# A graph layer on one core: the last slot keys turned in the feature split, dense work from the first group

## The chip, the cores and the metric

One core of one Trainium2 chip runs the kernel. The metric is the device time of one execution in microseconds; of several executions the median is given.

## What is computed

A graph network layer over 12,500 nodes of 128 features and 200,000 edges that are sorted by destination. Each edge has a source, a destination and one of nine types. `_layernorm` subtracts the mean of a row and divides by its standard deviation.

```python
src_h = h[src] @ W_msg.T + b_msg
msg = src_h + edge_embed[clip(edge_type, 0, 8)]
messages = segment_sum(msg, dst, num_segments=12500)
h_new = gru_cell(messages, h, W_ih, W_hh, b_ih, b_hh)
out = _layernorm(x + h_new)
```

Destinations are drawn as 12500 times the square of a uniform number, so low nodes have many edges each and high nodes few.

## The kernel before

The kernel sums raw features (and counts of types) per destination first and applies the weights to the sums. It has two ways to sum, by destination.

**The sparse way** serves nodes from 3584 up. Its edges come as 736 tiles of 128, in 184 groups of four. GpSimd gathers the source rows of a tile from memory by an indirect DMA (L604) into a ring of 23 tiles, and waits on `s_used` for the tile that stood in the slot. VectorE builds a one-hot of destinations and one of types (L844, L846), TensorE multiplies both with the gathered rows into one PSUM bank `psg` (L1061 for groups below 22, L1065 after, then L1069), and VectorE adds the bank into a ring of sums (L891). Group g + 1 may write `psg` only once that addition of group g is through.

**The dense way** serves nodes below 3584. All features stay in SBUF as three bf16 parts, `xs`. The edges are cut into 1748 slots of 128 edges of a few nodes. A slot has three keys per edge: `lo` and `key` (in `prm`) and `sort`. From them VectorE builds one-hots for four slots at a time (L862, L865, L868), TensorE multiplies them into `psb` (a "B" item, L1082), ScalarE copies each finished PSUM bank, four nodes wide, to SBUF (L1213), and for a finished block of 128 nodes TensorE multiplies the matrix with `xs` (an "F" item, L1097, in 49 parts of two matmuls).

**The split phase** stands ahead of both: 25 units of four feature tiles, each passing TensorE (L970, L973, L979) and ScalarE (L1147, L1153) in turn, give `xs`. SyncE writes `xs` out as `x_split` (L546) when the flag is known, for the gathers of the later groups. Beside the units VectorE finds the slots' edges, and `dense_keys(k)` (L688 to L698) makes the keys of a piece of slots: pieces 0 and 1 hold four columns of 128 slots, piece 2 holds six. TensorE turns keys by matmuls with an identity, `turn(a)` at L992, four columns at a time, the fourth time two. ScalarE copies what is turned from PSUM (`turned(a)`, L1163 and L1166). Turns 0 and 1 follow units 15 and 18. A matmul at L1002, after unit 21, adds up what VectorE has checked; VectorE makes the `flag` of it (L750 to L752), and every engine reads it before the main phase begins.

**The order of the main phase** is a list, `ITEMS`, which `schedule()` writes in Python and which TensorE, VectorE and ScalarE each walk. It puts one "G" and one "GA" item per group, and dense units between them so far as their share of the total keeps behind `pace((g - LEAD) / (GROUPS - REST - LEAD))`, from group `LEAD` on. With `LEAD = 4` the first B stands in group 4, one of 1748, and the first F in group 9. The item "keys" (piece 2) stands ahead of group 0, the items "turn" (turns 2 and 3) in groups 1 and 2, and "weights", a stage of fp32 matmuls and a chain on VectorE that prepares the biases, in group 10. VectorE prepares one-hots ahead of use: groups 0 and 1, and then the first two lots of four slots, are prepared before it comes to the addition of group 0.

Of the kernel before, what the change touches and what calls it, by code (L numbers as in the profile page):

```python
# [6 lines left out]
P = 128  # L7
# [20 lines left out]
NB = 3  # L28
# [18 lines left out]
PRE = UNITS + 2  # L47
LEAD = 4
REST = 6
# [5 lines left out]
SHIFT = 5  # L55
TURN_AT = (15, 18)
SUM_AT = 21
TURNS_AT = (1, 2)
EARLIER = 0.15
# [133 lines left out]
def schedule():  # L193
# [40 lines left out]
    for g in range(GROUPS):  # L234
        ub.append(float(clear - W))
        top = place(min(E, T0 * P + 512 * (g + 1)))
        assert top + MARGIN < clear - W
        chunks = [[("G", g)]]
        if g == 0:
            items.append(("keys", len(PIECES) - 1))  # L240
        if g in TURNS_AT:
            chunks.append([("turn", len(TURN_AT) + TURNS_AT.index(g))])
        if g == READY:
            chunks.append([("weights",)])
        if not units and late is None and not first:
            late = done
        n = STEPS[late is not None]
        outs = [step(g, place(T0 * P + 512 * g)) for _ in range(n)]
        lb.append(float(low))
        while units and g >= LEAD and spent <= total * pace((g - LEAD) / (GROUPS - REST - LEAD)):  # L250
            w, u = units.pop(0)
            spent += w
            chunks.append([u])
            if u[0] == "C":
                added += 1
        chunks[min(1, len(chunks) - 1)].append(("GA", g))
        if g >= GROUPS - 2:
            chunks = [[("end",)]] + outs + [[("hh", NBLK - 1, NBLK - 1)] if g == GROUPS - 1 else []] + chunks
            outs = []
        for c in range(len(outs)):  # L260
            chunks[max(min(1, len(chunks) - 1), (len(chunks) * c) // n)].extend(outs[c])
        for c in chunks:
            items += c
# [52 lines left out]
def gnn_kernel(nc, x, xT, xN, srcT, dstT, typT, dstG, dstC, dstS, dstB, rec, srcA, typA, dstE, low, table, masks,  # L316
               wmsg, bmsg, embT, wihT, whhT, bih, bhh, out):
    ctx = ExitStack()
    with ctx:
# [98 lines left out]
        def late(n):  # L418
# [30 lines left out]
                 "s_bi s_em s_cn s_used s_oh s_acc s_ok s_kd s_eb s_fd s_toh s_tr s_sl s_main "  # L449
                 "s_e18 s_wp s_wc s_xn s_hh s_pm s_rz s_t2 s_n s_y s_mv s_sd s_ln s_xc s_p1 s_xe s_p2 s_xl s_xw s_nid s_sc s_tt s_xt").split()  # L450
        S = {n: sem(n) for n in names}
# [185 lines left out]
        def _(v):  # L637
# [109 lines left out]
            v.wait_ge(s_rec[2], 16 * (PIECES[2][1] - PIECES[2][0]))  # L747
            v.tensor_tensor(badc[:, 0:J], recI[:, :, P - 1, 1], end, ALU.is_lt).then_inc(S["s_bad"], 1)
            v.wait_ge(S["s_sum"], 1)
            link(v.tensor_reduce(vi[:, 3:4], psg[0:1, 2 * P:2 * P + J + 2], AX, ALU.add))  # L750
            link(v.tensor_reduce(vi[:, 4:5], vi[:, 0:4], AX, ALU.add))
            v.tensor_scalar(flag[:, :], vi[:, 4:5], 100.0, None, ALU.min).then_inc(S["s_fl"], 1)  # L752
            v.wait_ge(S["s_z"], 8)
            v.wait_ge(S["s_fl"], 1)
# [79 lines left out]
            with v.If(bad == 0):  # L834
# [3 lines left out]
                def prepare(it):  # L838
# [11 lines left out]
                    elif it[0] == "B":  # L850
                        a = it[1]
                        group = range(a, min(a + OB, SLOTS_N))
                        if a % (4 * P) == 0:
                            v.wait_ge(S["s_te"], 3 * (a // (4 * P) + 1))
                        if a >= KB:
# [24 lines left out]
                def consume(it):  # L880
# [17 lines left out]
                    elif it[0] == "S":  # L898
                        q = it[1]
                        v.wait_ge(S["s_fd"], q + 1)  # L900
                        if q:
                            v.wait_ge(S["s_tt"], q)
                        v.tensor_reduce(added[:, :], psf[:, 0:3 * H].rearrange("p (c f) -> p f c", c=3), AX, ALU.add
                                        ).then_inc(S["s_sc"], 1)
                    elif it[0] == "keys":
                        dense_keys(it[1])
                    elif it[0] == "weights":
                        weights()
                    elif it[0] in STAGES or it[0] == "zero":
                        final(*it, False, BEFORE[(it[0], it[1])] if it[0] == "cn" else seen)  # L910
# [15 lines left out]
            with v.Else():  # L926
                cnt[0] = linked
                settle()
                for done in ("s_p1", "s_p2", "s_xe", "s_xl"):
                    v.wait_ge(S[done], UNITS)  # L930
                v.wait_ge(S["s_prm"], len(PIECES) - 1)
                v.wait_ge(S["s_te"], 3 * len(TURN_AT))
                link(v.memset(mem[:, 0:2 * ACC], 0.0))
# [28 lines left out]
        def _(pe):  # L962
# [21 lines left out]
            def turn(a):  # L984
                j0, j1 = TURNS[a]
                pe.wait_ge(S["s_prm"], min(a, len(PIECES) - 1) + 1)
                for c in range(3):
                    i = 3 * a + c
                    if i >= NB:
                        pe.wait_ge(S["s_te"], i - NB + 1)  # L990
# [56 lines left out]
            with pe.If(bad == 0):  # L1047
                pe.wait_ge(S["s_id"], 2)
                for it in ITEMS:
# [22 lines left out]
                    elif it[0] == "B":  # L1072
                        e = it[1]
                        _, _, k, tiles = DS[e]
                        if e == 0:
                            pe.wait_ge(S["s_te"], 3 * len(TURNS))
                        if e % OB == 0:
# [27 lines left out]
                    elif it[0] == "T":  # L1105
# [3 lines left out]
                                  ).then_inc(S["s_tt"], 1)  # L1109
                    elif it[0] == "turn":  # L1110
                        turn(it[1])
                    elif it[0] == "weights":
# [20 lines left out]
        def _(act):  # L1133
# [34 lines left out]
            for t in range(PRE):  # L1168
# [4 lines left out]
                if t == 10:  # L1173
                    act.wait_ge(S["s_sg"], 16)
                    act.dma_start(gm.rearrange("p a g -> p (a g)"), g_d.partition_broadcast(P)).then_inc(S["s_bg"], 16)
                if t in TURN_AT:
                    turned(TURN_AT.index(t))
# [22 lines left out]
            with act.If(bad == 0):  # L1200
                for it in ITEMS:
                    if it[0] == "turn":
                        turned(it[1])
                    elif it[0] == "B":
                        e = it[1]
# [20 lines left out]
            with act.Else():  # L1226
                act.wait_ge(S["s_prm"], len(PIECES) - 1)
                act.dma_start(slow_idx, srcA).then_inc(S["s_si"], 16)
# [79 lines left out]
```

## Time and profile before

| | |
|---|---|
| median of 3 executions | 1085.25 us (1083.91 to 1088.41) |
| profiled execution, from its first to its last instruction | 1255.1 us |
| TensorE (PE) busy in it | 1037.9 us, 83% |
| VectorE (DVE) busy | 859.2 us, 68% |
| GpSimd (POOL) busy | 733.5 us, 58% |
| ScalarE (ACT) busy | 660.5 us, 53% |
| mean granted TensorE clock | 0.926 |

Of the profiled execution the span is what the page gives; it gives no time beside it. The times of the trace are those of that execution, which is 170 us longer than the median. Busy time of matmuls is modelled. A wait that is put down to "remote" was released by something that the records don't show. The split phase ends at 100.7 us of the span and group 0 begins at 101.4 us.

### The profile page before, as it was taken

The numbers are of one execution on the slowest core, as the hardware profiler recorded it, in microseconds if no ns is written. First come the engines' busy times: TensorE is split into PE (matmuls) and PEld (weight loads), VectorE is DVE, ScalarE is ACT, GpSimd is POOL, SyncE is SP. The second block draws the span as 40 slices with busy tenths as digits, with TensorE's granted clock in tenths as the row PEclk, the third lists the DMA queues.
The fourth block names the chain that finished last, engine by engine and source line by source line (L and its number), as shares of the span: only waits on it lengthen the run. The fifth ranks groups of instructions, "written<-read, shape, count | busy, mean of one in ns | idle before, by whom it ended". The sixth has DMA issues, their size and how long they took to land.

```text
span 1255.1 us, 23526 instructions
## 1 busy us (share of the span) xinstructions
PE 1037.9 (83%) x8411; PEld 656.5 (52%) x8411; DVE 859.2 (68%) x2699; ACT 660.5 (53%) x1283; POOL 733.5 (58%) x779
## 2 busy tenths in 40 slices
PE   5456677888888988989889989889888888888884
PEld 2124354555555555556556656555555555555552
DVE  8413557677776877868777767777876777676644
ACT  4243404455655555656666656555655556554622
POOL 7725645665566666666666666566666666566640
PEclk9566568999999999999999999999998999999996
DMA  8529311222222322322333223223323233332321
GB/s 244 159 79 310 107 33 53 78 77 74 74 77 79 91 77 77 91 78 77 82 83 92 79 78 92 74 79 92 90 77 89 76 89 83 86 92 80 83 81 28
DMA packets 94565, 114.23 MB, mean 91 GB/s; under 512 B 19820, under 2 KB 80616, under 8 KB 94441
## 3 DMA queue, kind: packets, MB, share of 16 engines
q0 software_dynamic: 35264, 73.19, 21.8%
q1 hardware_dynamic: 57320, 37.79, 10.2%
q10 hardware_dynamic: 1856, 1.66, 0.5%
q8 instruction: 70, 1.15, 0.4%
q14 instruction: 55, 0.44, 0.1%
HBM read 96.56 MB, written 16.00 MB: 90 GB/s over the span
## 4 chain that ended last, share of the span: by engine, by line
PE 64%; issue 10%; DVE 9%; ACT 7%; another core or an unknown queue 7%; DMA 1%; SPq 1%; DVEq 0%; ACTq 0%
PE psf L1097 28%; PE psb L1082 14%; PE pAB L1026 5%; PE psg L1065 4%; PE pAB L1040 4%; ACT mem L1213 3%; DVE ohl L868 2%; PE pAB L1043 2%; DVE ohk L862 2%; PE psg L1069 2%; PE psf L1102 1%; DMA arena<-in_x 1%; ACT mem L1153 1%; DVE ohk L865 1%
## 5 line engine op out<-in xcount | busy, mean ns | idle before, releaser
L604 POOL DMA_INDIRECT xg<-x_split,idx x648 | 616.1, 951 | 392.1 <-PE psg L1069 151.0
L1213 ACT CAST mem<-psb 128x432 f16<-128x432 f32 x896 | 426.7, 525 | 398.4 <-PE psb L1082 300.8
L1097 PE MATMUL psf<-mem 128*128 128x384 bf16 (+1 forms) x2744 | 618.4, 330 | 13.6 <-issue 6.8
L1082 PE MATMUL psb<-ohk,ohl 128*128 128x108 bf16 (+3 forms) x1865 | 421.6, 264 | 97.9 <-issue 57.4
L862 DVE TENSOR_TENSOR ohk<-table_bank,prm 128x392 bf16<-128x392 f16 (+3 forms) x437 | 271.0, 620 | 108.6 <-PE psb L1082 69.1
L1097 PEld LDWEIGHTS psf<-mem 128*128 128x128 f16 (+1 forms) x2744 | 240.4, 99 | 131.3 <-issue 34.9
L1082 PEld LDWEIGHTS psb<-ohk,ohl 128*128 128x128 bf16 x1865 | 173.6, 100 | 251.3 <-issue 116.4
L868 DVE TENSOR_TENSOR ohl<-table_bank,prm 128x512 bf16<-128x512 f16 x437 | 180.8, 414 | 0.0
L891 DVE TENSOR_TENSOR mem<-mem,psg 128x136 f32 (+9 forms) x184 | 54.9, 298 | 168.4 <-remote 106.8
L604 POOL DMA_INDIRECT xg<-in_x,idx x88 | 84.2, 957 | 76.3 <-PE psg L1069 44.7
L865 DVE TENSOR_TENSOR ohk<-table_bank,sort 128x40 bf16<-128x40 f16 (+3 forms) x437 | 106.5, 244 | 0.0
L1065 PE MATMUL psg<-ohs,xg 128*128 128x76 bf16 (+8 forms) x1944 | 92.9, 196 | 5.1 <-issue 5.1
L1065 PEld LDWEIGHTS psg<-ohs,xg 128*128 128x128 bf16 x1944 | 84.4, 97 | 19.7 <-issue 6.3
L844 DVE TENSOR_TENSOR ohs<-rel,table_bank 128x272 f32<-128x272 f16 (+9 forms) x184 | 81.0, 440 | 0.8 <-DVE flag L752 0.8
L1026 PE MATMUL pAB<-whh,xb 128*128 128x384 f32 x188 | 73.4, 514 | 0.0
L1198 ACT ACT_TABLE_LOAD x48 | 61.6, 1283 | 0.9
L1190 ACT ACT_TABLE_LOAD x48 | 61.6, 1283 | 0.9
L1069 PE MATMUL psg<-ohs,tohb 128*128 128x68 bf16 (+9 forms) x736 | 55.8, 198 | 0.9 <-issue 0.9
L1040 PE MATMUL pAB<-wihc,mem 128*128 128x384 f32 x136 | 50.3, 492 | 2.3 <-DVE cnts L784 2.3
L1190 ACT ACTIVATE arena<-pAB 128x512 f32<-128x512 f32 x47 | 28.1, 597 | 43.3 <-PE pAB L1043 30.4
L1043 PE MATMUL pAB<-emw,cnts 128*128 128x512 f32 x94 | 44.2, 551 | 0.0
L1026 PEld LDWEIGHTS pAB<-whh,xb 128*128 128x128 f32 x188 | 34.6, 197 | 16.2 <-issue 2.2
(148 smaller groups left out, 808.4 us busy)
## 6 DMA issues: line engine op xcount, KB each, us to landing
xg<-x_split,idx POOLq DMA_INDIRECT x648
x_split<-mem SPq DMA_DIRECT2D x24, 384.0 KB
xb<-in_xT SPq DMA_DIRECT2D x49, 128.0 KB
arena<-in_x SPq DMA_DIRECT2D x24, 256.0 KB
arena<-in_xN SPq DMA_DIRECT2D x47, 128.0 KB
out<-spill SPq DMA_DIRECT2D x19, 128.0 KB
out<-arena SPq DMA_DIRECT2D x144, 8.0 KB
out<-arena SPq DMA_DIRECT2D x15, 128.0 KB
```

The lines of the kernel that those rows point to most:

```text
L604: pool.indirect_dma_start(out=xg[:, p % RING, :] if split else xg32(p % RING), out_offset=None, in_=x_d if split else x, in_offset=bass.In ...
L844: v.tensor_tensor(onehots(g)[0], rel[:, g, :].unsqueeze(2).to_broadcast([P, G, w]), count_up[:, 0:w].unsqueeze(1).to_broadcast([P, G, w]), ...
L862: v.tensor_tensor(nodes[:, :, :, HT:HC], numbers[:, :, HT:HC].unsqueeze(1).to_broadcast([P, k, m, HI]), key[:, a:a + k, :].unsqueeze(2).to ...
L865: v.tensor_tensor(nodes[:, :, :, 0:HT], numbers[:, :, HT:2 * HT].unsqueeze(1).to_broadcast([P, k, m, HT]), sort[:, a:a + k].unsqueeze(2).u ...
L868: v.tensor_tensor(ohl[:, a % KB:a % KB + k, :].rearrange("p k (c t) -> p k c t", t=2), count_up[:, 0:P].rearrange("p (c t) -> p c t", t=2) ...
L1026: ins = pe.matmul(pAB[:, s, H:4 * H], xb[:, i % 2, s * P:(s + 1) * P], whh[:, :], start=True, stop=False, skip_group_check=True)
L1040: pe.matmul(pAB[:, s, 0:3 * H], sums[:, s * P:(s + 1) * P], wihc[:, :], start=False, stop=False, skip_group_check=True)
L1065: ins = pe.matmul(g2[:, 0, 0:w], xg[:, p % RING, c * H:(c + 1) * H], oh16[:, j, :], start=(j == 0 and c == 0), stop=(j == G - 1 and c == 2 ...
L1082: ins = pe.matmul(psb[:, bank % NB, held * HC:(held + m) * HC], ohl[:, e % KB, :], ohk[:, e % KB, d * HC:(d + m) * HC], start=(k == 0), st ...
L1097: pe.matmul(psf[:, 0:3 * H], Bb[q % 2][0:kk, HT + h, :], xs[0:kk, h, :, :].rearrange("p c f -> p (c f)"), start=(h == 0), stop=(h == HI - ...
L1190: act.activation(rz[:, :, :], pAB[:, :, H:3 * H], ACT.Sigmoid).then_inc(S["s_rz"], 1)
L1213: act.copy(Bb[q % 2][:, :, n:n + MOST], psb[:, bank % NB, 0:MOST * HC].rearrange("p (d h) -> p h d", h=HC)).then_inc(S["s_eb"], 1)
```

## The change

`LEAD` goes from 4 to 0, so that dense units are spread from group 0 on. `dense_keys(2)` moves on VectorE from the start of the main phase to the wait for the flag's sum. Turns 2 and 3 move on TensorE to follow units 21 and 22; their copies move from ScalarE in the main phase to VectorE, behind the flag and ahead of its reading, and signal a new semaphore `s_tv`. The sum of the flag (L1002) moves from unit 21 to unit 19.

```diff
-LEAD = 4
+LEAD = 0
...
-TURN_AT = (15, 18)
-SUM_AT = 21
-TURNS_AT = (1, 2)
+TURN_AT = (15, 18, 21, 22)
+BY_ACT = 2
+SUM_AT = 19
...
-        if g == 0:
-            items.append(("keys", len(PIECES) - 1))
-        if g in TURNS_AT:
-            chunks.append([("turn", len(TURN_AT) + TURNS_AT.index(g))])
...
             v.tensor_tensor(badc[:, 0:J], recI[:, :, P - 1, 1], end, ALU.is_lt).then_inc(S["s_bad"], 1)
+            dense_keys(2)
             v.wait_ge(S["s_sum"], 1)
...
             v.tensor_scalar(flag[:, :], vi[:, 4:5], 100.0, None, ALU.min).then_inc(S["s_fl"], 1)
+            for a in range(BY_ACT, len(TURNS)):
+                j0, j1 = TURNS[a]
+                cols, n = slice(j0 * P, j1 * P), (j1 - j0) * P
+                for c in range(3):
+                    i = 3 * a + c
+                    v.wait_ge(S["s_tm"], i + 1)
+                    if c < 2:
+                        v.tensor_copy(prm[:, c, cols, :], psb[:, i % NB, 0:n].unsqueeze(2).to_broadcast([P, n, 2])
+                                      ).then_inc(S["s_tv"], 1)
+                    else:
+                        v.tensor_copy(sort[:, cols], psb[:, i % NB, 0:n]).then_inc(S["s_tv"], 1)
...
-                        if a % (4 * P) == 0:
-                            v.wait_ge(S["s_te"], 3 * (a // (4 * P) + 1))
+                        t = a // (4 * P)
+                        if a % (4 * P) == 0 and t < BY_ACT:
+                            v.wait_ge(S["s_te"], 3 * (t + 1))
+                        elif a % (4 * P) == 0:
+                            v.wait_ge(S["s_tv"], 3 * (t - BY_ACT + 1))
...
-                    if i >= NB:
+                    if i >= NB + 3 * BY_ACT:
+                        pe.wait_ge(S["s_tv"], i - NB - 3 * BY_ACT + 1)
+                    elif i >= NB:
                         pe.wait_ge(S["s_te"], i - NB + 1)
...
                         if e == 0:
-                            pe.wait_ge(S["s_te"], 3 * len(TURNS))
+                            pe.wait_ge(S["s_te"], 3 * BY_ACT)
+                            pe.wait_ge(S["s_tv"], 3 * (len(TURNS) - BY_ACT))
...
-                if t in TURN_AT:
+                if t in TURN_AT[:BY_ACT]:
                     turned(TURN_AT.index(t))
```

TensorE at the end of the split phase, from the flag's sum on, before (L970, L973 and L979 are one unit; `psb<-pid` is a turn):

```order
L1002 MATMUL psg<-ohl,one 1x16
L970 MATMUL pAB<-arena,ident 128x512
L973 MATMUL pAB<-mem,nid 128x512
L979 MATMUL pAB<-mem,nid 128x512
L970 MATMUL psf<-arena,ident 128x512
L973 MATMUL psf<-mem,nid 128x512
L979 MATMUL pAB<-mem,nid 128x512
L970 MATMUL pAB<-arena,ident 128x256
L973 MATMUL pAB<-mem,nid 128x256
L979 MATMUL psf<-mem,nid 128x512
L979 MATMUL pAB<-mem,nid 128x256
L493 TENSOR_LOAD flag
```

and after (line numbers are those of the changed kernel: L980, L983 and L989 a unit, L1004 a turn, L1014 the sum):

```order
L1004 MATMUL psb<-pid,mem 128x128 x12
L980 MATMUL pAB<-arena,ident 128x512
L983 MATMUL pAB<-mem,nid 128x512
L989 MATMUL pAB<-mem,nid 128x512
L1004 MATMUL psb<-pid,mem 128x128 x6
L980 MATMUL psf<-arena,ident 128x512
L983 MATMUL psf<-mem,nid 128x512
L989 MATMUL pAB<-mem,nid 128x512
L980 MATMUL pAB<-arena,ident 128x256
L983 MATMUL pAB<-mem,nid 128x256
L989 MATMUL psf<-mem,nid 128x512
L989 MATMUL pAB<-mem,nid 128x256
```

Two turns now stand in the last five units, and the sum has left this stretch; it stands two units ahead of it.

TensorE in the first groups of the main phase, before (`psg<-ohs,xg` begins a group):

```order
L1061 MATMUL psg<-ohs,xg 128x52 x4
L1069 MATMUL psg<-ohs,tohb 128x52 x4
L1061 MATMUL psg<-ohs,xg 128x52 x4
L1069 MATMUL psg<-ohs,tohb 128x52 x4
L992 MATMUL psb<-pid,mem 128x128 x12
L1061 MATMUL psg<-ohs,xg 128x52 x4
L1069 MATMUL psg<-ohs,tohb 128x52 x4
L992 MATMUL psb<-pid,mem 128x128 x6
L1061 MATMUL psg<-ohs,xg 128x52 x4
L1069 MATMUL psg<-ohs,tohb 128x52 x4
L1061 MATMUL psg<-ohs,xg 128x52 x4
L1069 MATMUL psg<-ohs,tohb 128x52 x4
```

and after (`psb<-ohk,ohl` is a B item):

```order
L1073 MATMUL psg<-ohs,xg 128x52 x4
L1081 MATMUL psg<-ohs,tohb 128x52 x4
L1095 MATMUL psb<-ohk,ohl 128x108
L1073 MATMUL psg<-ohs,xg 128x52 x4
L1081 MATMUL psg<-ohs,tohb 128x52 x4
L1095 MATMUL psb<-ohk,ohl 128x108 x12
L1073 MATMUL psg<-ohs,xg 128x52 x4
L1081 MATMUL psg<-ohs,tohb 128x52 x4
L1095 MATMUL psb<-ohk,ohl 128x108 x3
L1095 MATMUL psb<-ohk,ohl 128x216 x8
L1073 MATMUL psg<-ohs,xg 128x52 x4
L1081 MATMUL psg<-ohs,tohb 128x52 x4
```

The turns are gone from groups 1 and 2, and the B items that began in group 4 begin in group 0.

VectorE from the flag's sum to the one-hots of groups 0 and 1, before:

```order
L750 TENSOR_REDUCE vi<-psg 1x1
L751 TENSOR_REDUCE vi<-vi 1x1
L752 TENSOR_SCALAR flag<-vi 1x1
L493 TENSOR_LOAD flag
L834 COMPARE_AND_BRANCH
L844 TENSOR_TENSOR ohs<-rel,table_bank 128x208
L846 TENSOR_TENSOR tohb<-typ,table_bank 128x72
L844 TENSOR_TENSOR ohs<-rel,table_bank 128x208
L846 TENSOR_TENSOR tohb<-typ,table_bank 128x72
L688 TENSOR_SCALAR mem<-mem 128x768
L689 SCALAR_TENSOR_TENSOR mem<-mem,ohl 128x768
```

and after, in the changed kernel's lines:

```order
L747 TENSOR_REDUCE vi<-psg 1x1
L748 TENSOR_REDUCE vi<-vi 1x1
L749 TENSOR_SCALAR flag<-vi 1x1
L757 CAST prm<-psb 128x1024 x2
L760 CAST sort<-psb 128x512
L757 CAST prm<-psb 128x512 x2
L760 CAST sort<-psb 128x256
L489 TENSOR_LOAD flag
L842 COMPARE_AND_BRANCH
L852 TENSOR_TENSOR ohs<-rel,table_bank 128x208
L854 TENSOR_TENSOR tohb<-typ,table_bank 128x72
L852 TENSOR_TENSOR ohs<-rel,table_bank 128x208
```

The seven instructions of the keys (two of them shown) have left this place for the one above the sum, and six copies from PSUM stand between the flag and its reading.

## Rows read from the trace of the kernel before

**Rows 1.** The page: busy time of the engines, and the granted clock in 40 slices.

```profile
PE 1037.9 (83%) x8411; PEld 656.5 (52%) x8411; DVE 859.2 (68%) x2699; ACT 660.5 (53%) x1283; POOL 733.5 (58%) x779
...
PEclk9566568999999999999999999999998999999996
```

**Rows 2.** Busy time by stage (from:to, length, busy us of each engine, PEclk, DMA share, GB/s).

```profile
101.40:117.30 15.90, 9.13 (x66) 8.69 (x67) 5.51 (x21) 3.77 (x6) 10.06 (x11) 0.60 1.07 349
117.30:152.50 35.20, 20.27 (x116) 14.31 (x117) 15.82 (x51) 10.44 (x22) 23.24 (x25) 0.50 0.54 173
152.50:179.40 26.90, 22.14 (x103) 13.11 (x103) 15.23 (x50) 4.42 (x10) 12.13 (x14) 0.56 0.13 32
179.40:183.10 3.70, 3.70 (x40) 2.92 (x38) 2.88 (x12) 0.52 (x1) 2.17 (x3) 0.98 0.15 38
400.00:1100.00 700.00, 624.05 (x5439) 406.28 (x5438) 521.73 (x1650) 412.86 (x807) 432.05 (x455) 0.98 0.31 83
```

**Rows 3.** Waits of other engines released by "remote" (us in total, times, longest).

```profile
DVE mem L891 <- remote: 106.8, 63, 6.5
...
ACT mem L1213 <- remote: 65.1, 21, 14.4
```

**Rows 4.** VectorE in order of time, 95 to 115 us (start, duration, operation, idle before).

```profile
95.72 0.16 DVE L750 TENSOR_REDUCE vi<-psg 1x1 f32<-1x16 f32 x1 [17.77 <-PE psg L1002]
...
97.05 0.37 DVE L844 TENSOR_TENSOR ohs<-rel,table_bank 128x208 f32<-128x208 f16 x1 [0.81 <-DVE flag L752]
...
97.90 0.69 DVE L688 TENSOR_SCALAR mem<-mem 128x768 int32<-128x768 int32 x1
...
102.66 0.55 DVE L698 TENSOR_TENSOR mem<-mem 128x768 f16<-128x768 f16 x1
...
114.34 0.26 DVE L891 TENSOR_TENSOR mem<-mem,psg 128x104 f32 x1 [6.52 <-remote]
```

**Rows 5.** TensorE in order of time: the split phase's end, and groups 1 to 12.

```profile
95.49 0.20 PE L1002 MATMUL psg<-ohl,one 128*1 128x16 f32 x2
...
97.01 1.10 PE L970 MATMUL psf<-arena,ident 128*128 128x512 f32 x2
...
104.90 1.92 PE L1061 MATMUL psg<-ohs,xg 128*128 128x52 f32 x8 [2.34 <-issue]
...
106.81 1.46 PE L992 MATMUL psb<-pid,mem 128*128 128x128 bf16 x12
...
109.95 0.82 PE L992 MATMUL psb<-pid,mem 128*128 128x128 bf16 x6
...
120.59 1.92 PE L1061 MATMUL psg<-ohs,xg 128*128 128x52 f32 x8 [1.11 <-issue]
...
131.00 1.92 PE L1061 MATMUL psg<-ohs,xg 128*128 128x52 f32 x8
...
158.50 0.82 PE L1097 MATMUL psf<-mem 128*128 128x384 bf16 x2 [0.57 <-ACT mem L1213]
...
179.48 1.10 PE L1061 MATMUL psg<-ohs,xg 128*128 128x52 f32 x8
180.42 0.27 PE L1069 MATMUL psg<-ohs,tohb 128*128 128x52 bf16 x4
```

**Rows 6.** ScalarE and VectorE reading PSUM: a turn's copies, and two reads of known length.

```profile
88.48 1.93 ACT L1163 CAST prm<-psb 128x1024 f16<-128x1024 f32 x2 [1.47 <-PE psb L992]
...
164.78 0.42 DVE L762 TENSOR_SCALAR wihc<-pAB 128x256 f32<-128x256 f32 x1 [6.59 <-PE pAB L1012]
165.12 0.28 DVE L763 TENSOR_SCALAR wihc<-pAB 128x128 f32<-128x128 f32 x1
```

**Rows 7.** Two stretches of 5 us around the bias stage, same columns as rows 2.

```profile
160.00:165.00 5.00, 5.00 (x20) 2.65 (x19) 0.22 (x1) 0.00 (x0) 2.22 (x3) 0.50 0.11 26
165.00:170.00 5.00, 1.79 (x13) 0.96 (x10) 4.79 (x14) 0.00 (x0) 1.65 (x2) 0.84 0.15 39
```

**Rows 8.** One of GpSimd's gathers, the second after group 0.

```profile
104.33 0.95 POOL L604 DMA_INDIRECT xg<-in_x,idx  x1 [0.30 <-issue]
```

More of the change, by code:

```diff
@@ L449, in gnn_kernel @@
                  "s_bi s_em s_cn s_used s_oh s_acc s_ok s_kd s_eb s_fd s_toh s_tr s_sl s_main "
-                 "s_e18 s_wp s_wc s_xn s_hh s_pm s_rz s_t2 s_n s_y s_mv s_sd s_ln s_xc s_p1 s_xe s_p2 s_xl s_xw s_nid s_sc s_tt s_xt").split()
+                 "s_e18 s_wp s_wc s_xn s_hh s_pm s_rz s_t2 s_n s_y s_mv s_sd s_ln s_xc s_p1 s_xe s_p2 s_xl s_xw s_nid s_sc s_tt s_xt s_tv").split()
         S = {n: sem(n) for n in names}
@@ L904, in consume @@
                                         ).then_inc(S["s_sc"], 1)
-                    elif it[0] == "keys":
-                        dense_keys(it[1])
                     elif it[0] == "weights":
@@ L930, in _ @@
                     v.wait_ge(S[done], UNITS)
-                v.wait_ge(S["s_prm"], len(PIECES) - 1)
-                v.wait_ge(S["s_te"], 3 * len(TURN_AT))
+                v.wait_ge(S["s_prm"], len(PIECES))
+                v.wait_ge(S["s_te"], 3 * BY_ACT)
+                v.wait_ge(S["s_tv"], 3 * (len(TURNS) - BY_ACT))
                 link(v.memset(mem[:, 0:2 * ACC], 0.0))
@@ L1109, in _ @@
                                   ).then_inc(S["s_tt"], 1)
-                    elif it[0] == "turn":
-                        turn(it[1])
                     elif it[0] == "weights":
@@ L1201, in _ @@
                 for it in ITEMS:
-                    if it[0] == "turn":
-                        turned(it[1])
-                    elif it[0] == "B":
+                    if it[0] == "B":
                         e = it[1]
@@ L1226, in _ @@
             with act.Else():
-                act.wait_ge(S["s_prm"], len(PIECES) - 1)
+                act.wait_ge(S["s_prm"], len(PIECES))
                 act.dma_start(slow_idx, srcA).then_inc(S["s_si"], 16)
```

## The prediction, made before the change was run

> **What bounds the kernel now.** I read the page first. TensorE is busy 83% of the span, VectorE 68%, and the clock is mostly full except in slices 1 to 6 [rows 1]. The stages then say where the change acts. From 400 to 1100 us TensorE is busy 624 of 700 us at clock 0.98: the long middle is bound by TensorE's work, which this change neither adds to nor takes from. The first stages differ. Groups 0 to 3, which hold no dense unit, take 15.9 us, and TensorE is busy 9.13 of them. Groups 4 to 8, with B items alone, take 35.2 us, busy 20.27, at clock 0.50. Groups 9 to 11, with the first F items and the bias stage, take 26.9 us at 0.56. Group 12 runs at 0.98 in 3.7 us [rows 2]. So a change at the start can gain TensorE's idle time there, and its time at the half clock, and nothing else.
>
> How far is this trace to be trusted? Its span of 1255.1 us is 170 us above the median of 1085.25 us. Part of its waits end with "remote": 106.8 us ahead of VectorE's additions and 65.1 us ahead of ScalarE's evictions [rows 3]. An example is the addition of group 2, which starts at 114.34 after 6.52 us idle [rows 4], although TensorE had gone on to turn 3, which stands behind group 2, at 109.95 [rows 5]. That is a completion seen about 4.2 us late. I take such waits to be largely absent from an undisturbed execution, so I make the sum twice, with and without them.
>
> **The change, part by part.**
>
> The keys. Seven instructions of VectorE run from 97.90 to 103.2 us [rows 4], 5.3 us in all. They move into the wait for the flag's sum, where VectorE sits idle for 17.77 us [rows 4]: they cost nothing there while that cover stands; if the records of piece 2 came 12 us later, they would delay the flag. What they cost before is what waited behind them, one-hots for the dense slots and then the addition of group 0. Group 1 on TensorE starts at 104.90, after 2.34 us idle [rows 5]. That idle time goes, up to 2 us.
>
> The turns. Of the 18 matmuls, 1.46 us stand ahead of group 2 and 0.82 us ahead of group 3 [rows 5]. The first delays group 2 by some 0.6 us, the rest lies beside the wait for the addition. ScalarE's copies of them lay beside idle time. Both of these gains lie inside the 15.9 us of groups 0 to 3 and are counted there.
>
> The copies on VectorE. No row shows VectorE copying a key. Two reads of PSUM cost 0.42 us for 256 elements and 0.28 us for 128 [rows 6], so about 0.14 us and 1.1 ns an element: 1.26 us for 1024 elements, 0.70 for 512, 0.42 for 256. Bounds for the large one are ScalarE's 0.97 us (1.93 for two [rows 6]) below and twice 0.70 us above; I take 1.26, from VectorE's own rows. Turn 2 is then 3.2 us, turn 3 1.8 us, 5.0 us together. Turn 2 can be read from about 95.8 us, since unit 21 ends where the sum now starts, 95.49 [rows 5]. Its third copy is through at 99.0. Turn 3 needs these banks, stands behind unit 22, and would otherwise start at 97.01 [rows 5]. TensorE therefore leaves it at 99.3, and four more unit steps, with ScalarE and SyncE's later writes of `x_split`, are queued behind it: **+2.3 us**. VectorE's last copy ends near 101, the flag is read in 0.81 us and the first one-hot takes 0.37 us [rows 4], a second less, so group 0's one-hots are ready near 102.5, inside that shift. The earlier sum (unit 19) only brings the flag before the copies. For bounds of this term: 0, if the units behind have slack, and 5.0, if all copies stand in line.
>
> ScalarE read a turn in 1.93 us for its two large copies [rows 6]. The Trainium skill (VectorE: DVE Perf Modes, Specifications) says that VectorE sits closer to SBUF and ScalarE closer to PSUM, which speaks against handing these copies to VectorE. The same page's table in "The TRN2 errata" would give (120 + 1024) / 0.96 GHz, an estimate of 1.19 us a large copy and 4.8 us for all six, and the term would stay within 0.2 us of mine; no run here shows the placement by itself.
>
> Dense work from group 0. Nothing is added: 1748 slots stay 1748. The order's first five groups now hold what groups 4 to 8 held, so I charge them the 35.2 us of that stage, and the stage of 15.9 us disappears [rows 2]. The four groups' sparse work has to be done elsewhere, in groups where TensorE is bound: 1.10 + 0.27 us a group at full clock [rows 5], over a busy share of 0.89, makes 1.5 us, 6.2 us for four. So the gain is 15.9 - 6.2 = **9.7 us**. Without the late completion in group 2 it is 11.7 - 6.2 = **5.5 us**. The groups in between are unchanged in kind, since a lead of four groups thins out to nothing by group 178. The end of the program is the same.
>
> GpSimd starts its refill behind group 0, so 2.3 us later. A gather takes 0.95 + 0.30 us [rows 8], and 713 of them make 891 us, which would end near 1000 us of a span of 1255: hidden.
>
> Sum: -9.7 + 2.3 = -7.4 us against the span, or -5.5 + 2.3 = -3.2 us without the late completion. Between the two I take -5: **1080 us** against the median of 1085.25 us, with 1077 to 1084 as this case's own range.
>
> **The rivals.**
>
> Nothing moves. The B items run at the half clock wherever among the first groups they stand, and TensorE was already busy 9.13 of 15.9 us [rows 2]; if the shift of 2.3 us becomes 5.0, the two cancel: 1085 us.
>
> The clock returns earlier. It is 0.50 from 160 to 165 us and rises after that, 7.4 us behind the first F at 158.50 [rows 5, 7]. Filled groups could bring that forward by several groups. The stage of groups 9 to 11 holds 22.14 us of TensorE's work at 0.56 [rows 2]; at 0.98 it would be 12.7 us, 9.5 less. With 8 of these: 1080 - 8 = 1072 us. Against it: TensorE was busy 5.00 of 5.00 us at 0.50 [rows 7], so being busy isn't enough at once. The Trainium skill (TensorE: Matmul & The Clock Gate, What's actually happening) holds that the throttled clock is the default and activity releases it; by that rule this case would be the likely one, and the trace agrees only in part, since a full stretch was still granted 0.50.
>
> Slower: the B items fall into the writes of `x_split`. Groups 0 to 4 now run from 104 to 139 us. Before, group 5, the one that met B items and these writes together, took from 120.59 to 131.00 [rows 5]. If each of the first five groups takes such 10.4 us, the stage takes 52 us in place of 35.2, which turns -7.4 into +9.4: 1094 us. It decides from a stage of 43 us on. For it speaks that DMA share in the first stage is 1.07 against 0.54 in the second [rows 2]; against it, that a B item moves no data by DMA.
>
> **How the numbers follow.** About 0.5%, 5.4 us, is what a measurement of this kernel can tell from no change. The forecast gets 0.50, of which 0.20 lie beyond 5.4 us. No effect gets 0.13, the earlier clock 0.20, all of it faster, and the slower case 0.17. So faster 0.40, same 0.43, slower 0.17. The range runs from 1070, below the clock's case, to 1089, in which the lesser half of the slower case lies.
>
> **What would show it.** The keys end near 84 us. Six copies of VectorE near 95.8 to 101 us, 1.26 us the large ones; TensorE's turn 3 ends near 99.3, and group 0 starts near 103.7. B items start in group 0, and the first F near 140 rather than 158.5. Full clock sets in near 150. The forecast is wrong if group 0 starts after 106, if the first five groups take over 43 us, or if the middle's busy time changes.

## The result: 1087.94 us, slower by 0.4%

| | before | after |
|---|---|---|
| median of 13 executions each | 1084.59 us (1082.31 to 1088.41) | 1087.94 us (1085.53 to 1093.65) |
| ratio, 95% interval | | 1.0038 [1.0023, 1.0052] |
| span of a profiled execution | 1083.2 us | 1085.5 us |
| mean granted TensorE clock in it | 0.967 | 0.971 |

The forecast was 1080 us, a gain. What came is a loss of some 3.3 us. It lies inside the 0.5% that I had called level and inside the stated range, but on the other side of the kernel before. That the range holds it is luck: its upper end was there for a slowdown beside the writes of `x_split`, which did not come.

One thing must be known to read the profiles: the kernel before took about 1085 us in some sessions and 1255 to 1276 us in others, on one and the same chip too. The profile from which the prediction was made, with its span of 1255.1 us, belongs to the second kind; the three times beside it belong to the first, which is called the ordinary level below. So the unchanged kernel was profiled again, as the first experiment, and the rows of before in this part are from there. All is at the ordinary level unless a sentence says otherwise.

The page of the kernel before, profiled again (busy time and granted clock):

```profile
span 1083.2 us, 23526 instructions
...
PE 989.8 (91%) x8411; PEld 649.6 (60%) x8411; DVE 856.0 (79%) x2699; ACT 667.9 (62%) x1283; POOL 734.0 (68%) x779
...
PEclk9877899999999999999999999999999999999996
```

The page of the changed kernel:

```profile
span 1085.5 us, 23527 instructions
...
PE 988.4 (91%) x8411; PEld 647.0 (60%) x8411; DVE 861.0 (79%) x2705; ACT 662.1 (61%) x1277; POOL 733.9 (68%) x779
...
PEclk9879899999999999999999999999999999999997
```

Against [rows 1] TensorE's share is 91%, not 83%, and of the clock's first ten slices four are below 9, not six. In the changed kernel the fourth slice is at 9, not 7, as the rival of the earlier clock had it, and yet the time is longer. So something later must give back what the start gained. Busy time by stretch answers to [rows 2]; the kernel before first (from:to, length, busy us and matmuls of TensorE, then of its weight loads, VectorE, ScalarE, GpSimd; clock, DMA share, GB/s):

```profile
69.00:124.00 55.00, 43.72 (x279) 32.21 (x279) 36.06 (x121) 17.93 (x38) 41.59 (x45) 0.66 0.69 222
124.00:250.00 126.00, 118.18 (x1030) 77.63 (x1030) 104.33 (x332) 72.74 (x146) 95.52 (x101) 1.00 0.32 84
250.00:1000.00 750.00, 720.71 (x6513) 483.50 (x6512) 623.30 (x1981) 500.10 (x963) 517.42 (x546) 1.00 0.35 93
```

The changed kernel:

```profile
69.00:124.00 55.00, 47.46 (x372) 34.38 (x373) 42.82 (x147) 15.72 (x35) 41.85 (x44) 0.81 0.67 214
124.00:250.00 126.00, 118.90 (x1020) 77.76 (x1019) 100.92 (x324) 78.42 (x157) 94.92 (x102) 1.00 0.31 84
250.00:1000.00 750.00, 711.01 (x6392) 475.93 (x6391) 614.80 (x1949) 488.90 (x944) 515.19 (x543) 0.99 0.35 93
```

From 69 to 124 us the changed kernel issues 93 matmuls more, at a clock of 0.81 against 0.66. Between 250 and 1000 us it issues 121 fewer, at 0.11 us each (711.01 / 6392) some 13 us of work. That is the middle, which the prediction had left out as unchanged. Its own sign of being wrong, "if the middle's busy time changes", has come true: 711.01 us against 720.71.

### The profile page after: what moved, and what is told of

It reads as the page before. It is cut to its first block, busy times and chain, and to the rows that moved or that the text cites. A ratio compares the mean times of both kernels' runs of the same rounds, so it can differ in the third digit from the quotient of the medians.

```text
span 1085.5 us, 23527 instructions
## 1 busy us (share of the span) xinstructions
PE 988.4 (91%) x8411; PEld 647.0 (60%) x8411; DVE 861.0 (79%) x2705; ACT 662.1 (61%) x1277; POOL 733.9 (68%) x779
## 4 chain that ended last, share of the span: by engine, by line
PE 75%; DVE 11%; ACT 6%; issue 4%; DMA 1%; POOL 1%; SPq 1%; DVEq 0%; ACTq 0%
PE psf L1110 35%; PE psb L1095 14%; PE pAB L1038 6%; PE pAB L1052 5%; PE psg L1077 5%; ACT mem L1222 3%; PE psg L1073 2%; PE psg L1081 2%; PE pAB L1055 2%; DVE ohl L879 1%; DVE ohk L661 1%; ACT L1209 1%; DVE ohk L873 1%; PE psf L1121 1%; DVE added L914 1%
## 5 line engine op out<-in xcount | busy, mean ns | idle before, releaser
L1110 PE MATMUL psf<-mem 128*128 128x384 bf16 (+1 forms) x2744 | 610.1, 328 | 14.6 <-ACT arena L1232 13.7
L1222 ACT CAST mem<-psb 128x432 f16<-128x432 f32 x896 | 433.7, 522 | 256.4 <-PE psb L1095 251.1
L1095 PE MATMUL psb<-ohk,ohl 128*128 128x108 bf16 (+3 forms) x1865 | 411.0, 261 | 21.3 <-ACT mem L1222 11.7
L1110 PEld LDWEIGHTS psf<-mem 128*128 128x128 f16 (+1 forms) x2744 | 238.9, 98 | 129.3 <-issue 27.0
L1038 PE MATMUL pAB<-whh,xb 128*128 128x384 f32 x188 | 71.0, 501 | 0.0
L1204 ACT ACTIVATE arena<-arena 128x256 f32<-128x256 f32 x47 | 19.7, 418 | 41.6 <-DVE arena L807 41.1
```

The source lines that it names most:

```text
L1038: ins = pe.matmul(pAB[:, s, H:4 * H], xb[:, i % 2, s * P:(s + 1) * P], whh[:, :], start=True, stop=False, skip_group_check=True)
L1095: ins = pe.matmul(psb[:, bank % NB, held * HC:(held + m) * HC], ohl[:, e % KB, :], ohk[:, e % KB, d * HC:(d + m) * HC], start=(k == 0), st ...
L1110: pe.matmul(psf[:, 0:3 * H], Bb[q % 2][0:kk, HT + h, :], xs[0:kk, h, :, :].rearrange("p c f -> p (c f)"), start=(h == 0), stop=(h == HI - ...
L1222: act.copy(Bb[q % 2][:, :, n:n + MOST], psb[:, bank % NB, 0:MOST * HC].rearrange("p (d h) -> p h d", h=HC)).then_inc(S["s_eb"], 1)
```

## The experiments

Each ratio is that to the kernel before, measured in the same session.

**The kernel before again, unchanged.**

> The kernel before, unchanged, for a second profile beside the first (span 1255.1 us, 170 us over the median). Theory D (the first profile was disturbed as a whole, the split phase too): span near 1085 us, group 0 starts near 67 to 69 us rather than 101.4, waits that end with remote nearly gone. Theory P (profiling itself stretches this kernel): span again 1200 us or more.

1085.06 us, span 1083.2, and no wait in the trace ends with "remote", where [rows 3] has 106.8 and 65.1 us of them. TensorE at the end of the split phase:

```profile
66.39 0.28 PE L979 MATMUL pAB<-mem,nid 128*128 128x256 bf16 x1 [0.37 <-ACT mem L1153]
67.83 1.07 PE L1061 MATMUL psg<-ohs,xg 128*128 128x52 f32 x8 [1.17 <-issue]
```

Group 0 starts at 67.83 us, not at about 101 as in [rows 2]. So the stages of 15.9 and 35.2 us on which the sum rested were lengths of the other level. Here groups 0 to 3 and groups 4 to 8 take 12.3 and 20.1 us (columns as above):

```profile
67.80:80.10 12.30, 9.01 (x66) 8.72 (x67) 5.96 (x21) 3.77 (x6) 9.25 (x11) 0.54 1.05 328
80.10:100.20 20.10, 18.10 (x116) 13.36 (x117) 15.74 (x51) 9.59 (x22) 15.23 (x17) 0.60 1.06 360
```

**The moves alone, with the old lead.**

> The changed kernel with LEAD back at 4: only keys, turns, copies and sum are moved. Theory A (the copies on VectorE hold up turn 3, and turn 3 the last units of the split phase, which costs more than the keys and turns gave back): slower than before by about 2 to 5 us, so the loss of 3.3 us is here. Theory B (the loss is in LEAD = 0): this kernel is 0 to 4 us faster than before.

```diff
-LEAD = 0
+LEAD = 4
```

1083.69 us, ratio 0.9996 [0.9983, 1.0009]. Moving the keys, the turns and the copies costs nothing that can be measured. The loss lies in the lead alone, the one line in which this kernel and the changed one differ: 1083.69 against 1087.94 us, 0.9996 against 1.0038 of the kernel before of their sessions, and the intervals don't meet.

The same stretches in this kernel, to be set beside the two tables above:

```profile
69.00:124.00 55.00, 43.66 (x269) 31.15 (x270) 34.06 (x114) 14.35 (x32) 41.81 (x44) 0.66 0.66 210
124.00:250.00 126.00, 118.12 (x1025) 77.29 (x1023) 104.73 (x332) 73.31 (x147) 95.21 (x102) 1.00 0.31 84
250.00:1000.00 750.00, 720.74 (x6527) 483.40 (x6526) 624.11 (x1989) 500.42 (x964) 519.55 (x548) 1.00 0.35 94
```

Counted from the program's start, this kernel has issued 1448 matmuls at 250 us and 7973 at 1000; the changed one 1534 and 7924. It is 86 ahead, then 49 behind. At 0.11 us each that is an estimate of 9.5 us ahead and 5.4 behind, and the spans lie 4.7 us apart (1080.8 and 1085.5).

What took it shows in TensorE's waits from 250 to 1000 us (us in total, times, longest). The moves alone:

```profile
PE psf L1121 <- DVE added L914: 10.6, 12, 1.5
PE psf L1110 <- ACT arena L1232: 9.7, 11, 1.7
PE psb L1095 <- ACT mem L1222: 4.9, 11, 1.1
PE psb L1095 <- DVE ohl L879: 3.0, 6, 1.3
```

The changed kernel:

```profile
PE psf L1121 <- DVE added L914: 14.6, 17, 2.0
PE psf L1110 <- ACT arena L1232: 12.4, 11, 3.0
PE psb L1095 <- ACT mem L1222: 8.2, 16, 1.3
PE psb L1095 <- DVE ohl L879: 3.2, 3, 1.5
```

28.2 against 38.4 us, on the same lines. The first two are the handoff between two blocks of dense nodes: VectorE's `added` feeds the transposition (L1121), ScalarE copies its result out of PSUM (L1232), and only then may the next block's F items write there (L1110). There are 28 such handoffs, and the list decides what lies around each. I added up TensorE's gaps that begin between 3 us before and 6 us after the start of each transposition: 30.6 us with the moves alone, 39.6 in the changed kernel. Of these, 23.0 and 30.1 us lie between 250 and 1000 us. That difference of 7.1 us is about three quarters of the 9.7 by which all of TensorE's idle time in this stretch is larger (39.0 against 29.3).

The longest one, in the changed kernel. ScalarE in order of time:

```profile
914.09 0.60 ACT L1201 ACTIVATE arena<-pAB 128x512 f32<-128x512 f32 x1 [1.91 <-PE pAB L1055]
914.58 0.51 ACT L1222 CAST mem<-psb 128x432 f16<-128x432 f32 x1
916.57 0.42 ACT L1204 ACTIVATE arena<-arena 128x256 f32<-128x256 f32 x1 [1.47 <-DVE arena L807]
916.89 0.24 ACT L1231 CAST cnts<-psf 18x128 fp32r<-18x128 f32 x1
917.03 0.25 ACT L1232 COPY arena<-psf 128x128 f32<-128x128 f32 x1
```

and TensorE beside it:

```profile
913.89 0.51 PE L1095 MATMUL psb<-ohk,ohl 128*128 128x108 bf16 x7
917.43 0.80 PE L1110 MATMUL psf<-mem 128*128 128x384 bf16 x2 [3.03 <-ACT arena L1232]
```

The copy that TensorE waits for is short, 0.24 + 0.25 us. But in ScalarE's order it stands behind a piece of the final stages (L1204) that has itself to wait for VectorE. ScalarE executes in order, so that wait is passed on to TensorE. I read the other waits over 1.7 us in this stretch too. The one that ends at 639.93 (2.12 us) has the same L1204 ahead of the copy. Those that end at 539.97 and 811.34 (1.82 and 1.74 us) have L1209 there, another piece of the final stages, whose load of an activation table takes 1.28 us. The one that ends at 602.73 (2.04 us) is a wait for VectorE's `added`, which stands there behind three one-hots and two operations of a final stage.

The idle time costs a second time. Four stretches of the changed kernel, each at the end of one of these waits, with the clock below 1 (columns as above):

```profile
600.00:605.00 5.00, 2.96 (x21) 2.17 (x19) 3.59 (x14) 1.90 (x6) 3.78 (x4) 0.80 0.30 82
640.00:645.00 5.00, 5.00 (x27) 2.85 (x27) 4.86 (x20) 1.78 (x4) 2.91 (x4) 0.66 0.59 162
810.00:815.00 5.00, 3.66 (x14) 2.20 (x15) 3.29 (x13) 2.11 (x6) 3.78 (x5) 0.66 0.46 118
915.00:920.00 5.00, 2.57 (x23) 1.93 (x24) 4.06 (x12) 1.22 (x5) 1.93 (x3) 0.71 0.22 62
```

Stepped through at 1 us, each is a stretch of about 3.4 us at the half clock (1.2 GHz), at the end of a wait of 2.04, 2.12, 1.74 and 3.03 us. In all it is 13.6 us at the half clock from 250 to 1000 us, where the moves alone have none: half of it, 6.8 us, of work is lost. 9.7 + 6.8 = 16.5 us is what the changed list costs in the middle, against the 15 us that 135 matmuls fewer (6527 - 6392) amount to. The kernel before, profiled again, has one such stretch itself, at 679.9 us.

**Other leads.**

> The changed kernel with LEAD = 2. Theory A: within 1.5 us of the changed kernel, 1087 to 1089 us. Theory B: half of the loss is back, so 1085 to 1086.5 us.

> The changed kernel with LEAD = 3. Theory S: the whole list shifts, so the time is a matter of where the blocks' ends fall: anywhere from 1081 to 1089 us, and it goes with TensorE's waits from 250 to 1000 us (28 us in the list of LEAD = 4, 38 us in that of LEAD = 0). Theory R: halfway between LEAD = 4 and LEAD = 2, 1085 to 1087 us, waits unchanged.

> The changed kernel with LEAD = 6, dense units later than before. Theory S: two groups' idle time more at the start (1 to 3 us) and blocks' ends elsewhere: 1082 to 1092 us, again with the waits. Theory R: faster than or equal to LEAD = 4, 1080 to 1084 us, since more of the dense units are behind the writes of x_split.

```diff
-LEAD = 0
+LEAD = 2    (then 3, and 6)
```

Lead 2: 1088.64, ratio 1.0047 [1.0025, 1.007]. Lead 3: 1082.59, 0.9983 [0.9972, 0.9994]. Lead 6: 1104.66, 1.0183 [1.0168, 1.0199]. Lead 2 took what its theory A had said, but not for its reason, since the moves cost nothing. Lead 3 fits theory S, which left a wide range. Lead 6 lies outside both of its ranges. Were the start all that matters, the time would rise steadily with the lead. From 0 over 2, 3 and 4 to 6 it reads 1.0038, 1.0047, 0.9983, 0.9996, 1.0183. TensorE's idle time around the 28 handoffs is, in the same order, 39.6, 39.7, 28.8, 30.6 and 37.7 us (30.4 in the kernel before): the three slower kernels are those with the long handoffs. That is a match over five lists, not a proof, and it doesn't give the sizes: lead 6 has shorter handoffs than lead 2 and is 16 us slower. It pays at the start too: from 69 to 124 us it is busy 41.81 us at clock 0.60, and it runs at the half clock for 93.3 us in all against 70.7 with the moves alone. Half of the difference, 11.3 us, and 11.9 us more of TensorE's idle time (104.0 against 92.1 in the whole span) make 23.2, and its span is 22.1 us longer.

**The copies back on ScalarE.**

> The changed kernel with turns 2 and 3 copied by ScalarE, in its own order behind units 21 and 22, as turns 0 and 1 are. ScalarE gets 4 us more between units in a phase where it is busy 9 to 10 of 10 us, VectorE loses 4.3 us of copies. Theory A (order of waits, not the engine, is what costs): group 0 starts 1 to 3 us later than in the changed kernel, and the time is 1 to 3 us longer, since the copies now stand wholly in the chain of ScalarE. If it is the other way, VectorE's copies were the dearer place.

```diff
-BY_ACT = 2
+BY_ACT = 4
...
-                v.wait_ge(S["s_tv"], 3 * (len(TURNS) - BY_ACT))
...
-                            pe.wait_ge(S["s_tv"], 3 * (len(TURNS) - BY_ACT))
```

1091.87 us, ratio 1.007 [1.0046, 1.0094]. The changed kernel had 1.0038 [1.0023, 1.0052] in another session, and the two intervals overlap at their ends. So VectorE was no worse a place for these copies, and probably the better one. Group 0's addition comes at 72.03 us against 70.82; that is the shift that theory A named, but it is no more than scatter, since group 0 starts anywhere from 67.80 to 71.49 us in kernels whose TensorE has the same instructions up to there. ScalarE took 1.93 us for the two large copies, which stood between its writes for the split's units; VectorE's are read below. The list is that of the changed kernel, and the half clock comes back in the same four stretches, at 0.73, 0.67, 0.66 and 0.66. Four out of four at the same places speak for the list and against chance, as far as two traces can.

**The early start with the old list behind it.**

> Dense units from group 0, but thinned so that at group 16 the list meets that of LEAD = 4; behind group 16 the two lists are the same item by item. Theory S (the early start fills idle time and gains, and LEAD = 0 loses it again because the formula moves the end of every block of 128 nodes against the other stages all the way to group 176): 4 to 9 us faster than the kernel with the moves alone, 1075 to 1080 us, and TensorE's waits from 250 to 1000 us back from 38.4 to about 28 us. Theory F (the early start has nothing to gain, TensorE was bound there too): 1083 to 1085 us. Theory R (dense units beside the writes of x_split are themselves slower, which is where LEAD = 0 lost): over 1085 us.

> The same with the meeting point at group 24. Theory S: 1075 to 1081 us, as with 16; the first blocks' ends move, 27 blocks' ends do not. Theory F: 1083 to 1085. Theory R: as the meeting at 16 or worse, since more dense units stand in the first groups (10 a group against 9).

```diff
-LEAD = 0
+LEAD = 4
+MERGE = 16
...
-        while units and g >= LEAD and spent <= total * pace((g - LEAD) / (GROUPS - REST - LEAD)):
+        share = pace((max(g, MERGE) - LEAD) / (GROUPS - REST - LEAD)) * min(g, MERGE) / MERGE
+        while units and spent <= total * share:
```

This is the most telling pair. Dense work begins at once, but from group 17 on (25 with `MERGE = 24`) the list is item by item the one of lead 4. 1075.99 us, ratio 0.992 [0.9907, 0.9934], and with 24 groups 1075.47 us, 0.9918 [0.9903, 0.9932]. Both beat both kernels, though one stretch of 3.4 us at the half clock (at 671.5 us) is left in the middle of the first of them. With `MERGE = 16`, from 250 to 1000 us:

```profile
250.00:1000.00 750.00, 721.82 (x6513) 484.25 (x6510) 624.68 (x1981) 498.84 (x960) 522.85 (x552) 1.00 0.35 94
```

and its waits there:

```profile
PE psf L1112 <- ACT arena L1234: 9.7, 11, 1.7
PE psf L1123 <- DVE added L916: 9.4, 11, 1.5
PE psb L1097 <- ACT mem L1224: 5.0, 11, 1.1
PE psb L1097 <- DVE ohl L881: 3.0, 6, 1.3
```

These are 27.1 us, the waits of the moves alone. The start's gain shows in when VectorE adds group 16. The moves alone, then this kernel:

```profile
144.41 0.26 DVE L902 TENSOR_TENSOR mem<-mem,psg 128x112 f32 x1
```

```profile
138.38 0.27 DVE L904 TENSOR_TENSOR mem<-mem,psg 128x112 f32 x1
```

Against the kernel before, profiled again, its additions are 7.7 to 8.2 us ahead at every group from 17 to 180, and 5.7 to 7.5 us ahead of those of the moves alone: what the start gained is kept. Those of the changed kernel swing between 2.0 us ahead and 7.7 behind, and the last is 2.6 behind.

What this pair does not show: up to group 16 its list isn't that of the changed kernel either. It is thinner there, some 9 B items a group against 12. Only a joint, the changed kernel's own start before the old list, separates the two.

**At the other level: a joint of the lists, and a wider spread of the handoffs.** Two questions were left: whether the list of lead 0 up to group 12, joined to the old one from 17 on, does as well, and whether the handoffs get shorter once more B items stand between the three steps of a handoff. The three sessions that were to tell this all fell on the level of 1255 to 1276 us.

> A splice of two lists: groups 0 to 12 item by item as the changed kernel (LEAD = 0), groups 13 to 16 with what is missing to LEAD = 4, groups 17 on item by item as with LEAD = 4. Theory S (the start of the changed kernel gains, its later list loses): 5 to 9 us faster than the moves alone, 1075 to 1079 us, TensorE's waits from 250 to 1000 us near 28 us. Theory R (the changed start itself costs): 1084 us or more.

> The changed kernel with the block handoffs spread: SETTLED from (0.02, 0.06, 0.10) to (0.02, 0.08, 0.14) and CLEAR from 0.17 to 0.22, so half as many again of B items stand between a block's reduction on VectorE (S), its turn (T), its copy on ScalarE (C) and the next block's F items. If the handoffs' idle time (39.6 us over 28 of them in the changed kernel, 30.6 with LEAD = 4) is what the list decides, it falls to 20 to 30 us and the time with it, to 1078 to 1084 us. If B items bunched without F items starve TensorE for one-hots, as VectorE makes them, waits on VectorE's one-hots take its place: 1086 to 1092 us.

> The same spread on the list that meets LEAD = 4 at group 16 (1075.99 us, handoffs 30.6 us idle). Theory of the handoffs: idle 20 to 28 us, 1068 to 1074 us. Starved for one-hots: 1076 to 1084 us.

> The splice of e8 again, since in its call the kernel before itself took 1254.65 us and the waits that are to be read were hidden among others. Where the kernel before takes about 1084 us: theory S 1075 to 1079 us, waits of TensorE from 250 to 1000 us near 28 us; theory R 1084 us or more.

> e9 again for the same reason. The handoffs' theory: idle time at the 28 handoffs falls from 39.6 us to 20 to 30, time 1078 to 1084 us. Starved for one-hots: 1086 to 1092 us. In the slow call it stood at 0.9931 of the kernel before, which speaks for the first.

> e10 again for the same reason. The handoffs' theory: 1068 to 1074 us, against 1075.99 for the same list without the spread. Starved for one-hots: 1076 to 1084 us.

> The changed kernel itself, as the yardstick of this call whatever level the chip runs at. At 1084 us for the kernel before: 1087 to 1089 us. At 1255 to 1275 us for the kernel before: unknown, 0.99 to 1.01 of it.

> Handoffs spread in the changed list, beside it in one call. The handoffs' theory: 3 to 9 us faster than the changed kernel of this call, with idle time at the handoffs down by as much. Starved for one-hots: equal or slower.

> Start of the changed kernel, list of LEAD = 4 from group 17 on. Theory S: 8 to 12 us faster than the changed kernel of this call; theory R: equal or slower.

> The thinned start that meets LEAD = 4 at group 16, as in e4. If it held at the level of 1084 us only, it is level with the kernel before here; if it is the list and no level of the chip, it stays 0.8% below the kernel before and 1.1% below the changed one.

The joint:

```diff
-        while units and g >= LEAD and spent <= total * pace((g - LEAD) / (GROUPS - REST - LEAD)):
+        late_share = pace((max(g, MERGE) - LEAD) / (GROUPS - REST - LEAD))
+        share = min(pace(g / (GROUPS - REST)), late_share) if g < MERGE else late_share
+        while units and spent <= total * share:
```

The spread, on the changed kernel or on that of `MERGE = 16`:

```diff
-SETTLED = (0.02, 0.06, 0.10)
-CLEAR = 0.17
+SETTLED = (0.02, 0.08, 0.14)
+CLEAR = 0.22
```

| kernel | session 1 (before 1254.65) | session 2 (1273.15) | session 3 (1276.12) |
|---|---|---|---|
| changed, as it is | | | 0.9897 [0.9842, 0.9952] |
| `MERGE = 16` | | | 0.9893 [0.9847, 0.9938] |
| joint | 0.9952 [0.992, 0.9983] | 0.9986 [0.9945, 1.0028] | 0.988 [0.9836, 0.9924] |
| changed, spread | 0.9931 [0.9904, 0.9958] | 0.9818 [0.9767, 0.9868] | 0.9882 [0.984, 0.9924] |
| `MERGE = 16`, spread | 0.9904 [0.9871, 0.9938] | 0.9943 [0.9909, 0.9977] | |

In the third session four kernels stand level, and the changed kernel, which loses 0.4% at the ordinary level, gains 1.0%. The joint and `MERGE = 16` were expected ahead of it there, and are not. Ratios move between these sessions by more than their intervals: the joint reads 0.9986 and 0.988, the changed kernel with the spread 0.9931 and 0.9818. So a verdict on lists from this level isn't to be carried over to the other, and these runs settle neither question. Nor did the spread shorten the handoffs there: the idle time around the 28 is 54.8 us in the changed kernel, and 62.5 to 65.9 in its three runs with the spread.

## Why the prediction was wrong, and where it was right

**The step that failed** is the sentence "The groups in between are unchanged in kind, since a lead of four groups thins out to nothing by group 178", with the one ahead of it that the long middle is something "which this change neither adds to nor takes from". The work there is the same; its order isn't. Setting the lead to 0 puts nine in ten of the dense units one to four groups earlier, and so shifts the 28 handoffs against the pieces of the final stages. That cost 9.7 us of idle time and 6.8 us of work at the half clock between 250 and 1000 us. With that stretch put back as it was (`MERGE = 16`), the time is 1075.99 us. That the loss arises in the middle is shown by the counts at 250 and 1000 us together with this swap; that the changed kernel's own start would gain as much before the old list is not shown, since the joint has no run at the ordinary level. That a long wait comes from a piece of the final stages ahead of the short step is read from the five longest, such as the one at 917 us, and the test of it, the spread, stays open.

**Dense work from group 0**, the term of 9.7 us (5.5 without late completions). A gain was there: the changed kernel is about 9.5 us of matmuls ahead of the moves alone at 250 us, and with the old list kept behind it the gain is 1083.69 - 1075.99 = 7.7 us. The size is close to the term by luck. The term was to be TensorE's idle time in groups 0 to 3, which is 15.9 - 9.13 = 6.8 us in [rows 2] but 12.30 - 9.01 = 3.3 us at the ordinary level. Up to 250 us, TensorE is idle 38.7 us with `MERGE = 16`, 41.1 with the moves alone and 42.2 in the kernel before: 2.4 to 3.5 us were filled. More of the gain is the clock. The mean granted clock of the six executions of `MERGE = 16` is 0.973, that of the 17 of the kernel before in the same session 0.969; over their spans that is an estimate of some 5 us of work.

**The earlier clock**, given 0.20. It came, on top of the filled idle time, as this rival had it. In the changed kernel the stretch from 69 to 124 us is at 0.81 against 0.66, and full clock is back at 84.20 us, before the first F at 93.12, against 100.88 with the moves alone. Up to 250 us it runs at the half clock for 34.1 us against 47.8, which is worth 6.8 us of the 8 that the rival had priced. It isn't so in every execution: the profiled one of `MERGE = 24` has 47.8 us too. What the rival left out is that the same clock can be lost again by a wait of 2 us later on.

**The keys at no cost.** Right, by a thin margin. The cover of [rows 4], 17.77 us of idle time, was 7.74 us in the kernel before at the ordinary level, and the earlier sum leaves less: TensorE's is through at 58.86 us, and the keys, from 54.30 on, last until 59.6. VectorE in the changed kernel, its last key and the flag's sum:

```profile
59.10 0.55 DVE L694 TENSOR_TENSOR mem<-mem 128x768 f16<-128x768 f16 x1
59.57 0.15 DVE L747 TENSOR_REDUCE vi<-psg 1x1 f32<-1x16 f32 x1
...
62.20 2.36 DVE L757 CAST prm<-psb 128x1024 f16<-128x1024 f32 x2 [2.12 <-PE psb L1004]
64.47 0.68 DVE L760 CAST sort<-psb 128x512 f16<-128x512 f32 x1
65.06 1.28 DVE L757 CAST prm<-psb 128x512 f16<-128x512 f32 x2
66.26 0.41 DVE L760 CAST sort<-psb 128x256 f16<-128x256 f32 x1
```

The reduction follows the last key without idle time, so the keys outlast the cover by 0.7 us. It costs nothing, since VectorE then waits 2.12 us for turn 2, and the flag is still 2.9 us earlier than before (59.94 against 62.80). The prediction had said that the flag is delayed if the records come 12 us later; here the cover itself was 10 us shorter.

**The copies.** A large one took 1.18 us where 1.26 were forecast from [rows 6]; all six 4.73 us against 5.0. The shift of group 0 by 2.3 us: it starts at 69.50 against 67.83, 1.67 later, with the turn waiting for the copies as described (the unit behind turn 2 starts at 62.44, the next one at 65.33, 2.89 us later against 1.40 before). But with the moves alone group 0 started at 67.80, and with lead 6 at 71.49, and TensorE's instructions up to there are the same in all three. So the scatter between executions is larger than this shift, and no cost of the term is shown. The ratio of 0.9996 for the moves alone is of the whole time: what they may cost in the split phase they give back in the first groups.

**The rival on the slower side** was the wrong one. It had the early B items run into the writes of `x_split`. It decides from 43 us on for the first five groups, and they took 18.4 us, from 69.50 to 87.86, in the midst of these writes. `MERGE = 16`, whose B items start as early, gains.

**The profile itself.** The prediction saw that the span was 170 us too long and set the "remote" waits apart, but it went on to take stage lengths from it. That span and median did not belong together was the warning.

## What to carry to other kernels

When a number sets where a static list begins to mix two streams of work, compare the two lists over their whole length, not at the start alone; to judge the start by itself, bend only the first items and keep the rest identical. Look for the places where two engines hand a buffer to and fro, and ask what stands ahead of the short copy in the queue of the engine that frees it. A gap of 2 us on TensorE can have a second price, a stretch at the half clock behind it. And where a gain comes out as large as its term, look whether it is made of what the term counted.

## What the runs showed of the hardware that was not expected

The half clock came back in the middle of a busy program, at the end of single waits of 1.74 to 3.03 us, for about 3.4 us each, at the same four places in two kernels with the same list. In the kernel before (at 679.9) and in `MERGE = 16` (at 671.5) it followed two waits of 1.25 to 1.35 and 0.72 us, 2 us apart. Waits of 1.82 us (changed kernel, at 539.97) and of 1.74 us (the moves alone, at 813.13) were not followed by one, so no rule is drawn from here.

The same kernel ran at 1084 us in some sessions and at 1255 to 1276 in others; on one chip its medians were 1084.44, 1254.65 and 1276.12 us. At the slower level "remote" ends many waits for TensorE's results, 120.3 us of VectorE's additions in the changed kernel, and TensorE is busy 653.01 of the 750 us from 250 to 1000 against 711.01 at the ordinary one. Why there are two levels stays open, and so does whether the joint of the lists and the wider spread help at the ordinary one.
